# Counts by ScalarE, stacked edge-weight products and a pair mask on GpSimd in a four-block graph kernel

## The chip, the cores and the metric

One NeuronCore of a Trainium2 chip runs the whole program. The metric is the device time of one execution in microseconds (us), and the median of several runs is what counts. The engines are TensorE (PE in the profile; its weight loads are PEld), VectorE (DVE), ScalarE (ACT), GpSimd (POOL) and SyncE (SP), which here only issues DMAs. Each engine works through its own list of instructions in order, and semaphores tie the lists together. GpSimd issues the indirect DMAs.

## The reference, cut to what matters

1250 nodes with 512 values each and 20000 edges, sorted by `dst`. Four blocks follow each other, each added to its input: an equivariant graph layer, a layer of 64 experts with routing, a graph attention net of four layers, and a feed-forward layer.

```python
# block 1, the edges
h = ssp(f_ij @ W1 + b1)                      # softplus minus log 2, 32 hidden values per edge
Wij = (h @ W2 + b2) * rcut_ij[:, None]       # 4 of the 6 weights per feature are used: 128 columns
# ... products of the gathered node values with Wf and the edge's directions ...
agg = segment_sum(edge, idx_i)
# block 3, in each layer and head
scores = einsum('ehd,ehd->eh', q[src], k[dst])
attn = softmax of the scores over the edges with the same src
out = segment_sum(attn[:, :, None] * v[dst], src)
```

The kernel does block 3 densely: scores of all 1250 x 1250 pairs, with the logarithm of the number of edges of a pair as a mask, and a very large value where a pair has no edge. So block 1 also counts edges per pair, for use in block 3.

## The kernel before

Stages follow each other, each with its own semaphores and a barrier of all engines at its end: constants, input projection, **edges**, node update, **expert norm**, **route**, **experts**, the first **rows stage**, and then attention and rows stages by turns. The rest is not touched.

**edges** handles 160 tiles of 125 edges as 40 groups (`g`) of 4 tiles (`EG`); four groups (`SG`) share one computation of the hidden values. The order is written out by hand on every engine.
- TensorE: `weigh(g + 1)` makes the weights of the next group in PSUM bank 5, a bias product (L521, float32r, 33 rows) and four fp32 products with 32 rows each (L523). Then `scatter(g, j)` sums the messages onto the nodes by products with one-hot rows, in a high and a low float32r part (L538). Once in four groups `turn` (L504) and `hidden` (L512) make the next hidden values.
- VectorE: `messages(g)` multiplies weights and gathered rows (L444 to L459), compares each edge's pair key with those of its tile (`same`, L466), masks that with a triangle (`prior`, L469), makes the low part (L473), and then the index work: `early` (L476), `kd` (L477), `late_cnt` (L478), `kf` (L480) and `late_idx` (L482). `hot` (L426) builds three of four one-hot rows, `act_sum` (L431) finishes the hidden values.
- ScalarE: `high` copies the messages' high part, `hot` makes the fourth one-hot row (L387, L389), `bend` and `softplus` the hidden values, `column_sums` (L398) sums expert weights for routing.
- GpSimd: `fetch` gathers the node rows of a group by four indirect DMAs (L338). `pair_adds` (L579) adds the counts of one tile to one of two count matrices in HBM (`pairs`), each an indirect DMA with accumulation. Addition `n` waits for the landing of addition `n - 2`. 60 are spread over the first 38 groups (`PACED_ADDS`), 68 are issued in the stage (`EARLY_ADDS`), and the others stand in later stages by the tuple `LATE`: 14 in node update, 12 in expert norm, 66 in experts.
- SyncE loads `keyrow` for each group and expert weights in pieces of 512 KB.

**route** computes on VectorE which expert each row goes to; GpSimd waits for the slots and scatters ten tiles of rows to HBM (L872), and the experts stage loads them back. SyncE loads 5 MB of expert weights at the same time. **experts**: GpSimd works through its 66 additions, waits for their landing and for the stored outputs, and gathers the outputs (L1075).

**First rows stage** (`rows_stage` with `masks`): norms of ten tiles of rows, then 24 units of queries and keys (`unit(n)`, L1437), then values (L1446). TensorE makes a unit, ScalarE takes it (`take(n)`), VectorE cuts the low part of a key (`finish(n)`, L1900). Between them stands the mask work per tile of 125 x 1250 counts: VectorE adds the two matrices and takes the maximum (L1908), ScalarE takes the logarithm (L1784) and a Relu with scale -1e28 (L1786), VectorE subtracts (L1914), SyncE stores. `COUNT_AT`, `LOG_AT` and `CAP_AT` give the unit after which each step stands. Counts of tiles 6 to 9 are loaded into buffers that earlier tiles leave; in SyncE's list the conditioning weights (`late`) stand between the loads of tile 7 and the store of mask 5, and SyncE waits there until they have landed.

## Time and profile before

| | |
|---|---|
| median of 3 runs | 2878.57 us (2877.28 to 2882.2) |
| the profiled execution | 2881.81 us, its span 2880.0 us |
| busy in the span | PE 2520.4, PEld 2166.2, DVE 1861.9, ACT 1396.8, POOL 1139.5 us |
| mean granted clock of TensorE | 0.945 of full speed |
| edges | first product of the stage's weights at 78.96 us, last scatter product until 543.1 us |
| route, experts | from 623.7 and from 663.9 us |
| first rows stage | from 943.7 us, value products from 1064.13 us |

Busy times are shares of engines that wait for each other, so they don't say what a change is worth; that is read from the stretch of time in which the changed work stands. A granted clock of 1.00 in a window is 2.4 GHz, one of 0.50 is 1.2 GHz. An instruction in a timeline has its start and its length; the difference of two starts is what it takes of its engine's time, since the next begins before the last one's end is through.

### The profile page before, as it was taken

The numbers are of one execution on the slowest core, as the hardware profiler recorded it, in microseconds if no ns is written. First come the engines' busy times: TensorE is split into PE (matmuls) and PEld (weight loads), VectorE is DVE, ScalarE is ACT, GpSimd is POOL, SyncE is SP. The second block draws the span as 40 slices with busy tenths as digits, with TensorE's granted clock in tenths as the row PEclk, the third lists the DMA queues.
The fourth block names the chain that finished last, engine by engine and source line by source line (L and its number), as shares of the span: only waits on it lengthen the run. The fifth ranks groups of instructions, "written<-read, shape, count | busy, mean of one in ns | idle before, by whom it ended". The sixth has DMA issues, their size and how long they took to land. (4 is left out here: it accounts for less than half of the span.)

```text
span 2880.0 us, 38762 instructions
## 1 busy us (share of the span) xinstructions
PE 2520.4 (88%) x13585; PEld 2166.2 (75%) x13585; DVE 1861.9 (65%) x3526; ACT 1396.8 (49%) x2764; POOL 1139.5 (40%) x850
## 2 busy tenths in 40 slices
PE   3999999746766668999999999989999989998999
PEld 3788878546556557887877877978978878877997
DVE  2899999564651745767646777457776367667862
ACT  1566566422245635655436655346654356544431
POOL 2788888853673002226003243013260022363420
PEclk9999999867878789999999999999999999999999
DMA  7444344238535752102221011111022030121101
GB/s 253 89 86 86 74 91 83 20 92 268 128 91 175 196 157 62 45 1 72 68 61 46 18 55 53 52 53 36 18 71 68 20 89 19 45 82 34 56 13 35
DMA packets 172076, 220.33 MB, mean 77 GB/s; under 512 B 111791, under 2 KB 120426, under 8 KB 164465
## 3 DMA queue, kind: packets, MB, share of 16 engines
q1 hardware_dynamic: 85134, 189.35, 22.6%
q0 software_dynamic: 86752, 28.51, 5.8%
q8 instruction: 111, 1.82, 0.3%
q14 instruction: 79, 0.65, 0.1%
HBM read 177.10 MB, written 40.15 MB: 75 GB/s over the span
## 5 line engine op out<-in xcount | busy, mean ns | idle before, releaser
L2185 POOL TENSOR_SCALAR prob<-prob,rden,linked 125x1250 f32<-125x1250 f32 x160 | 223.5, 1397 | 955.6 <-DVE rden L2152 955.6
L579 POOL DMA_INDIRECT pairs<-late_cnt,late_idx x160 | 351.1, 2195 | 125.5 <-DMA pairs<-late_cnt,late_idx 75.7
L2103 ACT CAST prob_high<-ps 125x375 fp32r<-125x375 f32 (+1 forms) x480 | 231.1, 503 | 267.1 <-PE ps L2065 261.8
L2144 DVE CUSTOM_DVE_ANT_0 prob<-ps,mask 125x1250 f32<-125x1250 f32 x160 | 233.0, 1456 | 130.1 <-PE ps L2041 109.1
L2157 DVE TENSOR_TENSOR prob_low<-ps,prob_high 125x375 fp32r<-125x375 f32 (+1 forms) x480 | 269.6, 585 | 46.6 <-ACT prob_high L2103 46.6
L338 POOL DMA_INDIRECT Hg<-h_rows,dsti x160 | 230.1, 1438 | 117.3 <-issue 94.0
L2054 PE MATMUL ps<-ident,prob 125*125 125x125 f32 x1600 | 252.3, 273 | 17.3 <-POOL prob L2185 10.7
L2054 PEld LDWEIGHTS ps<-ident,prob 125*125 125x125 f32 x1600 | 232.3, 187 | 29.7 <-POOL prob L2185 22.9
L538 PE MATMUL ps<-onehot,mhi 125*128 125x512 f32 (+1 forms) x960 | 245.7, 364 | 6.1 <-DVE onehot L426 5.9
L538 PE MATMUL ps<-onehot,mlo 125*128 125x512 f32 (+1 forms) x960 | 238.8, 357 | 0.0
L2095 ACT ACTIVATE prob<-prob,top 125x1250 f32<-125x1250 f32 x160 | 214.7, 1342 | 46.3 <-DVE top L2144 37.6
L2065 PE MATMUL ps<-prob_high,v_high 125*128 125x376 f32 (+1 forms) x480 | 211.1, 440 | 4.6 <-ACT qT L2107 3.0
L2041 PE MATMUL ps<-k_high,q_high 128*125 128x512 f32 (+1 forms) x480 | 173.9, 362 | 28.5 <-DVE q_low L2133 19.0
L538 PEld LDWEIGHTS ps<-onehot,mhi 125*128 125x128 f32 x960 | 158.4, 191 | 42.6 <-issue 13.4
L538 PEld LDWEIGHTS ps<-onehot,mlo 125*128 125x128 f32 x960 | 157.5, 191 | 28.2
L2041 PE MATMUL ps<-k_low,q_high 128*125 128x512 f32 (+1 forms) x480 | 172.5, 359 | 0.0
L2041 PE MATMUL ps<-k_high,q_low 128*125 128x512 f32 (+1 forms) x480 | 171.6, 358 | 0.0
L2065 PE MATMUL ps<-prob_low,v_high 125*128 125x376 f32 (+1 forms) x480 | 169.0, 352 | 0.0
L2065 PE MATMUL ps<-prob_high,v_low 125*128 125x376 f32 (+1 forms) x480 | 169.0, 352 | 0.0
L426 DVE TENSOR_SCALAR onehot<-iota_n,srcf 125x1250 fp32r<-125x1250 int16 x120 | 121.0, 1030 | 24.3 <-PEq L71 12.1
L2041 PEld LDWEIGHTS ps<-k_high,q_high 128*125 128x125 f32 x480 | 90.9, 189 | 50.3 <-DVE q_low L2133 20.7
L2330 POOL TENSOR_SCALAR neg<-raw,qsc 128x128 bf16<-128x128 f32 x132 | 78.6, 614 | 119.3 <-DVEq L2352 119.3
(442 smaller groups left out, 5952.4 us busy)
## 6 DMA issues: line engine op xcount, KB each, us to landing
mask<-mask_d SPq DMA_DIRECT2D x40, 546.9 KB
sg_wd<-L_ffn_Wd SPq DMA_DIRECT2D x32, 512.0 KB, 7.2
w_ring<-L_ffn_Wd SPq DMA_DIRECT2D x16, 1024.0 KB, 14.8
w_ring<-L_ffn_Wu SPq DMA_DIRECT2D x16, 1024.0 KB, 5.8
pairs<-zeros POOLq DMA_DIRECT2D x18, 625.0 KB, 25.2
keyrow<-keys_d SPq DMA_DIRECT2D x40, 244.1 KB
kept<-g_d SPq DMA_DIRECT2D x40, 224.0 KB
g_d<-kept SPq DMA_DIRECT2D x30, 224.0 KB
```

The costliest lines, as they stand in the source:

```text
L338: nc.gpsimd.indirect_dma_start(Hg[:, g % 2, j, :, :].rearrange("p c f -> p (c f)"), None, h_rows[:, :], bass.IndirectOffsetOnAxis(dsti[:, ...
L426: v.tensor_scalar(onehot[:, j, :], T.iota_n[0:P, :], srcf[:, column(g, j):column(g, j) + 1], None, ALU.is_equal).then_inc(hot_ready, 1)
L538: ins = nc.tensor.matmul(agg_chunk(T, a, c), part[:, u, j, a * 128:(a + 1) * 128], onehot[:, j, n0:n0 + nn], start=first and k == 0 and c < 2,
L579: nc.gpsimd.indirect_dma_start(pairs[a][:, :], bass.IndirectOffsetOnAxis(T.E.late_idx[:, c:c + 1], 0), T.E.late_cnt[:, c:c + 1], None, com ...
L2041: ins = nc.tensor.matmul(S(u)[0:P, n0:n0 + nn], M.qr[x][:, b % 2, i * P:(i + 1) * P], M.k[y][:, h, n0:n0 + nn], start=n == 0, stop=n == 2)
L2054: ins = nc.tensor.transpose(T.ps[0:P, 3 + s % 4, i * P:(i + 1) * P], M.prob[:, (FIRST[b] + i) % RING, j * P:(j + 1) * P], T.ident[0:P, 0:P])
L2065: ins = nc.tensor.matmul(T.ps[:, 7, 0:w], M.v[x][:, j, h * DH:(h + 1) * DH], M.pt[y][:, s % 3, 0:w], start=j == 0 and n == 0, stop=j == NT ...
L2095: s.activation(M.prob[:, u % RING, :], M.prob[:, u % RING, :], ACT.Exp, bias=M.top[:, u % RING:u % RING + 1], scale=-1.0, accum_out=M.den[ ...
L2103: s.copy(M.pt[0][:, n % 3, 0:w], T.ps[0:P, 3 + n % 4, 0:w]).then_inc(high, 1)
L2144: v.tensor_tensor_reduce(M.prob[:, r, :], S(u)[0:P, 0:N], M.mask[:, it % MASKS, :], 1.0, 3.0e38, ALU.add, ALU.min, M.top[:, r:r + 1]).then ...
L2157: v.tensor_tensor(M.pt[1][:, n % 3, 0:w], T.ps[0:P, 3 + n % 4, 0:w], M.pt[0][:, n % 3, 0:w].bitcast(F32), ALU.subtract).then_inc(low, 1)
L2185: nc.gpsimd.tensor_scalar(M.prob[:, r, :], M.prob[:, r, :], M.rden[:, r:r + 1], T.linked[:, it:it + 1], ALU.mult, ALU.mult).then_inc(norme ...
```

## The change

1. **Edge weights.** The hidden values of a group are split in a high and a low part and stacked by three DMAs per group on 98 rows: high, low, high, and two rows of ones. The weights stand against them as high, high, low and the two parts of the bias. One float32r product per tile replaces bias product and fp32 product. ScalarE and VectorE prepare the stacked weights at the stage's start.
2. **Index work.** `same` and `prior` become bf16. ScalarE sums the counts of each tile (`counts`), VectorE computes `kd` once for all tiles and `kf`, `late_idx` once in four groups.
3. **Additions.** They start with group 8: 40 up to group 37, 52 in the stage. Eight now stand in route, ahead of the scatters, and 74 in experts.
4. **Pair mask.** GpSimd adds the counts, compares and subtracts. ScalarE takes the logarithm alone, and its accumulated sum tells whether a row has an edge. VectorE does one small comparison in the end.

```diff
@@ -32,8 +32,10 @@
 SG = 4
-EARLY_ADDS = 68
-PACED_ADDS = 60
+EARLY_ADDS = 52
+PACED_ADDS = 40
+PACE_FROM = 8
+STACK = 8
@@ -292,24 +294,28 @@
         pre = sb("pre", [128, EG * P]); sa = sb("sa", [128, EG * P]); se = sb("se", [128, EG * P])
-        hT = sb("hT", [128, 2, EG * P])
+        hT = sb("hT", [128, EG * P]); h_hi = sb("h_hi", [128, 2, EG * P], F32R); h_lo = sb("h_lo", [128, 2, EG * P], F32R)
+        stack = sb("h_stack", [3 * FF + 2, STACK, EG * P], F32R); w_stack = sb("w_stack", [3 * FF + 2, 128], F32R)
...
         onehot = sb("onehot", [P, EG, N], F32R); away = sb("away", [P, N]); minus = sb("minus", [P, ET])
-        keyrow = sb("keyrow", [P, 2, EG, P]); same = sb("same", [P, EG, P]); prior = sb("prior", [P, EG, P])
+        keyrow = sb("keyrow", [P, 2, EG, P]); same = sb("same", [P, 2, EG, P], BF16); prior = sb("prior", [P, EG, P], BF16)
+        lowerb = sb("lowerb", [P, P], BF16); tally = sb("tally", [P, EG, P], BF16)
...
         wd_src = A["L0_ffn_Wd"]
-        early = sb("early", [P, EG]); kd = sb("kd", [P, EG]); kf = sb("kf", [P, EG])
+        early = sb("early", [P, 2, EG, SG]); kd = sb("kd", [P, ET]); kf = sb("kf", [P, EG * SG])
...
         names = ("wd_in0 wd_in1 wd_in2 wd_in3 summed keyrow_in0 keyrow_in1 hg_in0* hg_in1* keyrow_free f_turned fT_ready h_made bent soft_step h_ready "
...
@@ -322,6 +328,18 @@
                                      keyrows_d[g // SG, g % SG:g % SG + 1, :, :].broadcast_to([P, EG, P])).then_inc(keyrow_in[g % 2], 16)
+                        if g == 0:
+                            for k in range(2):
+                                sp.dma_start(w_stack[3 * FF + k:3 * FF + k + 1, :].bitcast(F32),
+                                             E.b2[32 * k:32 * k + 1, 0, :].bitcast(F32)).then_inc(b2_in, 16)
+                        if g % SG == 0:
+                            sp.wait_ge(h_split, g // SG + 1)
+                            for r in range(SG):
+                                if g + r >= STACK:
+                                    sp.wait_ge(w_made, g + r - STACK + 1)
+                                for k, part in enumerate((h_hi, h_lo, h_hi)):
+                                    sp.dma_start(stack[k * FF:(k + 1) * FF, (g + r) % STACK, :].bitcast(F32),
+                                                 part[r * FF:(r + 1) * FF, g // SG % 2, :].bitcast(F32)).then_inc(st_in[(g + r) % STACK], 16)
@@ -345,10 +363,12 @@
                             fetch(g + 2)
-                        more = PACED_ADDS * (g + 1) // NG if g < NG - 2 else EARLY_ADDS - 4 * (NG - 1 - g)
-                        pool.wait_ge(idx_ready, more // EG + 1)
-                        pair_adds(pool, nc, T, pairs, n, more)
-                        n = more
+                        if g >= PACE_FROM:
+                            more = PACED_ADDS * (g + 1 - PACE_FROM) // (NG - PACE_FROM) if g < NG - 2 else EARLY_ADDS - 4 * (NG - 1 - g)
+                            pool.wait_ge(idx_ready, (more - 1) // (EG * SG) + 1)
+                            pool.wait_ge(tallied, EG * SG * ((more - 1) // (EG * SG) + 1))
+                            pair_adds(pool, nc, T, pairs, n, more)
+                            n = more
@@ -388,6 +408,15 @@
 
+                    def counts(g):
+                        act.wait_ge(keyrow_free, g + 1)
+                        if g >= 1:
+                            act.wait_ge(tallied, EG * g)
+                        for j in range(EG):
+                            c = column(g, j)
+                            s.activation(tally[:, j, :], same[:, g % 2, j, :], ACT.Copy,
+                                         accum_out=E.late_cnt[:, c:c + 1]).then_inc(tallied, 1)
+
@@ -396,6 +425,10 @@
                             s.activation(junk[:, k, :], wd[:, l % WRING, i, k, :], ACT.Copy, accum_out=T.E.tsum[:, e, k:k + 1]).then_inc(summed, 1)
+                    s.copy(w_stack[0:3 * FF, :], E.w2[0:3 * FF, :, :].rearrange("p k f -> p (k f)")).then_inc(w_stacked, 1)
+                    s.activation(stack[3 * FF:3 * FF + 2, :, :],
+                                 T.zeros[3 * FF:3 * FF + 2, 0:EG * P].unsqueeze(1).broadcast_to([2, STACK, EG * P]), ACT.Identity,
+                                 bias=T.ones[3 * FF:3 * FF + 2, 0:1]).then_inc(w_stacked, 1)
@@ -411,6 +444,7 @@
                         hot(g)
+                        counts(g)
@@ -428,7 +462,14 @@
                         dve.wait_ge(soft_step, 2 * q + 2)
-                        v.scalar_tensor_tensor(hT[:, q % 2, :], sa[:], -LOG2, pre[:], ALU.add, ALU.add).then_inc(h_ready, 1)
+                        if q >= 2:
+                            for r in range(SG):
+                                dve.wait_ge(st_in[(SG * q + r) % STACK], 48 * (q // 2))
+                        v.scalar_tensor_tensor(hT[:], sa[:], -LOG2, pre[:], ALU.add, ALU.add).then_inc(h_ready, 1)
+                        dve.wait_ge(h_ready, q + 1)
+                        step(v.tensor_copy(h_hi[:, q % 2, :], hT[:]))
+                        settle()
+                        v.tensor_tensor(h_lo[:, q % 2, :], hT[:], h_hi[:, q % 2, :].bitcast(F32), ALU.subtract).then_inc(h_split, 1)
@@ -463,25 +504,32 @@
                         dve.wait_ge(keyrow_in[u], (g // 2 + 1) * 16)
-                        step(v.tensor_tensor(same[:], keyrow[:, u, :, :], kcol.unsqueeze(2).broadcast_to([P, EG, P]), ALU.is_equal))
+                        if g >= 2:
+                            dve.wait_ge(tallied, EG * (g - 1))
+                        step(v.tensor_tensor(same[:, u, :, :], keyrow[:, u, :, :], kcol.unsqueeze(2).broadcast_to([P, EG, P]), ALU.is_equal))
...
                         v.sem_inc(keyrow_free, 1)
-                        step(v.tensor_tensor(prior[:], same[:], T.lower[:].unsqueeze(1).broadcast_to([P, EG, P]), ALU.mult))
+                        step(v.tensor_tensor(prior[:], same[:, u, :, :], lowerb[:].unsqueeze(1).broadcast_to([P, EG, P]), ALU.mult))
...
                         settle()
-                        step(v.tensor_reduce(early[:], prior[:], AX.X, ALU.add))
-                        step(v.tensor_scalar(kd[:], kcol, T.iota_p[:, 0:1], None, ALU.subtract))
-                        step(v.tensor_reduce(E.late_cnt[:, tiles(g)], same[:], AX.X, ALU.add))
-                        settle()
-                        step(v.scalar_tensor_tensor(kf[:], early[:], 0.0, kd[:], ALU.is_equal, ALU.mult))
-                        settle()
-                        step(v.tensor_scalar(E.late_idx[:, tiles(g)], kf[:], T.iota_p[:, 0:1], None, ALU.add))
-                        settle()
-                        v.sem_inc(idx_ready, 1)
+                        q, r = divmod(g, SG)
+                        step(v.tensor_reduce(early[:, q % 2, :, r], prior[:], AX.X, ALU.add))
+                        if r == SG - 1:
+                            c = slice(EG * SG * q, EG * SG * (q + 1))
+                            settle()
+                            step(v.scalar_tensor_tensor(kf[:], early[:, q % 2, :, :].rearrange("p j r -> p (j r)"), 0.0, kd[:, c],
+                                                        ALU.is_equal, ALU.mult))
+                            settle()
+                            v.tensor_scalar(E.late_idx[:, c], kf[:], T.iota_p[:, 0:1], None, ALU.add).then_inc(idx_ready, 1)
+                    dve.wait_ge(w_stacked, 1)
+                    v.tensor_tensor(w_stack[2 * FF:3 * FF, :], E.w2[2 * FF:3 * FF, :, :].rearrange("p k f -> p (k f)"),
+                                    w_stack[2 * FF:3 * FF, :].bitcast(F32), ALU.subtract).then_inc(w_stacked, 1)
+                    step(v.tensor_copy(lowerb[:], T.lower[:]))
+                    step(v.tensor_scalar(kd[:], key[:], T.iota_p[:, 0:1], None, ALU.subtract))
@@ -512,16 +560,15 @@
                     def weigh(g):
-                        q, r = divmod(g, SG)
-                        rows = slice(r * FF, (r + 1) * FF)
-                        if r == 0:
-                            pe.wait_ge(h_ready, q + 1)
+                        pe.wait_ge(st_in[g % STACK], 48 * (g // STACK + 1))
+                        if g == 0:
+                            pe.wait_ge(w_stacked, 3)
+                            pe.wait_ge(b2_in, 32)
...
                             pe.wait_ge(w_free, g)
-                        nc.tensor.matmul(T.ps[0:P, 5, :], E.one33[:], E.b2[:].rearrange("p j c -> p (j c)"), start=True, stop=False)
                         for j in range(EG):
-                            ins = nc.tensor.matmul(T.ps[0:P, 5, j * 128:(j + 1) * 128], hT[rows, q % 2, j * P:(j + 1) * P],
-                                                   E.w2[rows, :, :].rearrange("p k f -> p (k f)"), start=False, stop=j == EG - 1)
+                            ins = nc.tensor.matmul(T.ps[0:P, 5, j * 128:(j + 1) * 128], stack[:, g % STACK, j * P:(j + 1) * P],
+                                                   w_stack[:], start=True, stop=True)
@@ -568,7 +615,7 @@
 
-LATE = (EARLY_ADDS, EARLY_ADDS + 14, EARLY_ADDS + 26, ET)
+LATE = (EARLY_ADDS, EARLY_ADDS + 14, EARLY_ADDS + 26, EARLY_ADDS + 34, ET)
@@ -867,6 +914,7 @@
                     g.iota(ecol[:], [[0, 1]], 0, 1, **kw).then_inc(made, 1)
+                    late_adds(pool, nc, T, pairs, 2)
@@ -1081,7 +1129,7 @@
                     g.memset(T.cw[:], 0.0).then_inc(c_made, 1)
-                    late_adds(pool, nc, T, pairs, 2)
+                    late_adds(pool, nc, T, pairs, 3)
@@ -1491,15 +1539,14 @@
         self.pair_c, self.pair_m = [free[name] for name in "abcdegjfhg"], [free[name] for name in "lmkjfhabcd"]
...
 
-COUNT_AT = (3, 4, 5, 6, 8, 9, 12, 13, 15, 17)
-LOG_AT = (4, 5, 6, 7, 9, 10, 13, 14, 16, 18)
-CAP_AT = (5, 6, 8, 9, 10, 11, 14, 16, 18, 19)
-TINY, BIG = 1.0e-18, 1.0e28
+LOG_AT = (4, 4, 5, 5, 6, 7, 14, 15, 20, 21)
+TINY, BIG = 1.0e-18, 1.0e30
+UNLINKED = (N - 0.5) * math.log(TINY)
@@ -1640,8 +1687,28 @@
                 if masks:
+                    def count(t):
+                        pool.wait_ge(pair_in[t], 64)
+                        nc.gpsimd.tensor_tensor(M.pair_c[t][:], M.pair_c[t][:], M.pair_m[t][:], ALU.add).then_inc(counted, 1)
+
+                    def mask(t):
+                        pool.wait_ge(logd, t + 1)
+                        nc.gpsimd.tensor_scalar(M.pair_m[t][:], M.pair_c[t][:], -1.0, BIG, ALU.is_lt, ALU.mult).then_inc(empty, 1)
+                        pool.wait_ge(empty, t + 1)
+                        nc.gpsimd.tensor_tensor(M.pair_c[t][:], M.pair_m[t][:], M.pair_c[t][:], ALU.subtract).then_inc(mask_made, 1)
                     nc.gpsimd.memset(M.tiny[:], TINY).then_inc(consts, 1)
-                    nc.gpsimd.memset(M.far[:], -BIG).then_inc(consts, 1)
+                    for t in range(6):
+                        count(t)
+                    for t in range(6):
+                        mask(t)
+                    count(6)
+                    count(7)
+                    mask(6)
+                    mask(7)
+                    count(8)
+                    count(9)
+                    mask(8)
+                    mask(9)
@@ -1779,11 +1846,10 @@
                     if t == 0:
-                        act.wait_ge(consts, 2)
+                        act.wait_ge(consts, 1)
                     act.wait_ge(counted, t + 1)
-                    s.activation(M.pair_c[t][:], M.pair_c[t][:], ACT.Ln, bias=M.tiny[0:P, :]).then_inc(logd, 1)
-                    act.wait_ge(logd, t + 1)
-                    s.activation(M.pair_m[t][:], M.pair_c[t][:], ACT.Relu, bias=M.far[0:P, :], scale=-BIG).then_inc(capped, 1)
+                    s.activation(M.pair_c[t][:], M.pair_c[t][:], ACT.Ln, bias=M.tiny[0:P, :],
+                                 accum_out=M.pair_top[:, t:t + 1]).then_inc(logd, 1)
@@ -1900,19 +1966,6 @@
 
-                def masking(n):
-                    for t in range(NT) if masks else ():
-                        if n == COUNT_AT[t]:
-                            c = M.pair_c[t][:]
-                            dve.wait_ge(pair_in[t], 64)
-                            v.tensor_tensor_reduce(c, c, M.pair_m[t][:], 1.0, 0.0, ALU.add, ALU.max,
-                                                   M.pair_top[:, t:t + 1]).then_inc(counted, 1)
-                    for t in range(NT) if masks else ():
-                        if n == CAP_AT[t]:
-                            c = M.pair_c[t][:]
-                            dve.wait_ge(capped, t + 1)
-                            v.tensor_tensor(c, M.pair_m[t][:], c, ALU.subtract).then_inc(mask_made, 1)
-
@@ -1935,15 +1988,11 @@
                 low(NT - 2)
-                masking(3)
...
                 low(NT - 1)
-                masking(4)
-                masking(5)
...
                     finish(n)
-                    masking(n)
@@ -1952,7 +2001,8 @@
                 if masks:
-                    v.tensor_scalar(T.linked[:], M.pair_top[:], 1.0, None, ALU.min).then_inc(spare, 1)
+                    dve.wait_ge(logd, NT)
+                    v.tensor_scalar(T.linked[:], M.pair_top[:], UNLINKED, None, ALU.is_gt).then_inc(spare, 1)
```

## Rows read from the trace of the kernel before

**Rows 1.** Windows: busy us of each engine, granted clock, DMA share, GB/s

```profile
300.00:350.00 50.00, 49.54 (x259) 40.46 (x258) 46.22 (x89) 30.37 (x77) 39.73 (x26) 1.00 0.44 89
```

**Rows 2.** Timeline of TensorE over four groups: start, length, work

```profile
305.63 0.50 PE L521 MATMUL ps<-b,one 33*125 33x512 f32 x1
306.06 1.13 PE L523 MATMUL ps<-w,hT 32*125 32x128 f32 x8
307.12 0.83 PE L538 MATMUL ps<-onehot,mhi 125*128 125x512 f32 x3
...
318.53 0.80 PE L538 MATMUL ps<-onehot,mhi 125*128 125x512 f32 x3 [0.42 <-DVE onehot L426]
...
351.15 0.50 PE L521 MATMUL ps<-b,one 33*125 33x512 f32 x1
```

**Rows 3.** Timeline of VectorE, index work and hidden values

```profile
304.62 0.54 DVE L477 TENSOR_SCALAR kd<-key,iota_p 125x4 f32<-125x4 f32 x1
304.75 0.66 DVE L478 TENSOR_REDUCE late_cnt<-same 125x4 f32<-125x500 f32 x1
...
306.02 1.85 DVE L426 TENSOR_SCALAR onehot<-iota_n,srcf 125x1250 fp32r<-125x1250 int16 x2
...
341.10 0.66 DVE L431 SCALAR_TENSOR_TENSOR hT<-sa,pre 128x500 f32<-128x500 f32 x1
```

**Rows 4.** Groups by line in the edge stage: busy us, mean ns

```profile
L538 PE MATMUL ps<-onehot,mlo 125*128 125x226 f32 x317 | 85.5, 270 | 0.0
...
L398 ACT ACTIVATE sg_junk<-sg_wd 128x128 f32<-128x128 f32 x228 | 67.2, 296 | 1.6 <-ACT sg_junk L398 0.4
L389 ACT ACTIVATE onehot<-away,ones 125x1250 fp32r<-125x1250 f32 x36 | 48.3, 1343 | 1.2
```

**Rows 5.** Timeline at the edge stage's start

```profile
78.22 0.68 DVE L431 SCALAR_TENSOR_TENSOR hT<-sa,pre 128x500 f32<-128x500 f32 x1 [8.12 <-ACT sa L374]
```

**Rows 6.** Timeline at its end: 13 additions, and TensorE's last products

```profile
509.75 2.17 POOL L579 DMA_INDIRECT pairs<-late_cnt,late_idx  x1 [0.30 <-issue]
...
540.32 1.97 POOL L579 DMA_INDIRECT pairs<-late_cnt,late_idx  x1 [0.30 <-issue]
542.35 0.75 PE L538 MATMUL ps<-onehot,mlo 125*128 125x512 f32 x3
```

**Rows 7.** GpSimd in route and experts (timeline), and windows of route

```profile
640.49 1.23 POOL L872 DMA_INDIRECT xs_d<-xf,r_slot  x1 [16.09 <-DVEq L945]
666.12 2.02 POOL L579 DMA_INDIRECT pairs<-late_cnt,late_idx  x1 [0.19 <-issue]
...
693.09 1.98 POOL L579 DMA_INDIRECT pairs<-late_cnt,late_idx  x1 [13.33 <-DMA pairs<-late_cnt,late_idx]
...
723.51 1.98 POOL L579 DMA_INDIRECT pairs<-late_cnt,late_idx  x1 [5.84 <-DMA pairs<-late_cnt,late_idx]
...
636.00:640.00 4.00, 4.00 (x40) 4.00 (x40) 1.01 (x3) 0.00 (x0) 0.00 (x0) 0.50 0.98 408
640.00:644.00 4.00, 4.00 (x40) 4.00 (x40) 0.14 (x1) 0.00 (x0) 2.90 (x3) 0.50 0.35 35
```

**Rows 8.** GpSimd's wait before the gather of the outputs (timeline)

```profile
916.95 1.27 POOL L1075 DMA_INDIRECT w_ring<-y_d,r_slot  x1 [29.77 <-DMA y_d<-xs]
```

**Rows 9.** GpSimd beside VectorE in the rows stage, and GpSimd's scaling

```profile
954.63 1.26 POOL L1624 TENSOR_TENSOR set_b_low<-set_b_raw,set_b_high 128x512 fp32r<-128x512 f32 x1 [2.82 <-ACT set_b_high L1733]
954.76 1.15 DVE L1873 SCALAR_TENSOR_TENSOR shift<-mv,rstd 125x1 f32<-125x1 f32 x1
...
L2185 POOL TENSOR_SCALAR prob<-prob,rden,linked 125x1250 f32<-125x1250 f32 x160 | 223.5, 1397 | 955.6 <-DVE rden L2152 955.6
```

**Rows 10.** Rows stage: waits, the store of mask 3, the first value product

```profile
PE ps L1437 <- DVE k_low L1900: 21.5, 4, 14.0
...
1009.20 0.30 SPq L141 DMA_DIRECT2D mask_d<-pair_d  x1
...
1064.13 1.09 PE L1446 MATMUL ps<-set_b_high,y_high 128*125 128x512 f32 x4
```

12 lines of the change are left out of this document (7 added, 5 removed).

## The prediction, made before the changed kernel ran

> **What bounds the kernel now.** I read the windows first, then the groups of instructions by line, then the timeline at each place that the diff touches. From 85 to 543 us the edge stage runs, and there the windows show TensorE busy 49.5 of 50 us and VectorE 46.2, ScalarE 30.4, GpSimd 39.7 [rows 1]. The timeline shows that both are the bound: from one edge-weight product to the one four groups later TensorE takes 45.52 us, 11.38 a group, and waits once in them, 0.42 us for a one-hot of VectorE [rows 2]; and VectorE's instructions follow each other without a gap of any size [rows 3]. So the stage speeds up only by what leaves both engines. Behind it lie stages of waits: the clock is 1.2 GHz (granted 0.50) and the DMA queues are full in the routing stage [rows 7], and in the first rows stage TensorE stands idle 21.5 us for VectorE's key splits [rows 10], which are queued behind mask work that waits for its counts. GpSimd's long lists of count additions end inside the stage where they stand, at some ends with little room [rows 6, 8].
>
> **Edge stage, TensorE.** A group's weights take 1.49 us, 305.63 to 307.12: one bias product and four fp32 products, each in two instructions [rows 2]. After: four single-pass products of 128 columns. The nearest rows: eight L523 instructions fill the 1.06 us between 306.06 and 307.12, 0.13 each, so four are 0.53; above lies the one-hot product of 226 columns, single-pass too, whose 270 ns from start to end make 1.08 for four [rows 2, 4]; below, half of 0.53, were a product bound by its columns alone. With the lead of 0.2 us that now stands before the block I take 0.75: 0.74 less a group (bounds 0.2 and 1.0).
>
> **Edge stage, VectorE.** By starts in the timeline the key difference takes 0.13 us, and the count reduction with the two index steps 1.27 up to the next one-hot, of which the reduction is 0.66 and the steps 0.61 [rows 3]. The first two leave, the steps come once in four groups: 0.13 + 0.66 + 0.75 x 0.61 = 1.25 us less. The product with the triangle passes over the same 500 elements as that reduction and now has bf16 operands: unchanged, or half, 0 to 0.3 less; I take 0.1, as every row here of such a pass has the full time. Added once in four groups: a copy, a subtraction of 500 columns and two drains, each instruction at most the 0.66 us of L431 [rows 3], 1.4 us, 0.35 a group. Net 1.0 less (0.8 to 1.2): 10.4 a group. The Trainium skill, VectorE: DVE Perf Modes, section What auto-detection actually checks, says that an operation whose tensors are all 16-bit with unit step gets the mode of two results a cycle; by it the triangle product falls by some 0.3 us and the group to 10.2. No row here has that form.
>
> **Edge stage, ScalarE and GpSimd.** ScalarE gets four counts a group, each like L398 at 0.296 us [rows 4]: 1.2 us more on 6.9, by its 30.4 of 50 us [rows 1]. In the group that also has the softplus (with two table loads 5.2 us) its copy for the message split comes about 1.5 us late; once in four groups, 0.1 to 0.4 us a group if nothing hides it. I take a period of 10.5 us, 0.85 less (0.5 to 1.0). Over the 37 groups up to the last fetch: 31.5 us. GpSimd has 4 fetches of 1.75 and 1.25 additions of 2.6 a group, 10.3 us: just inside.
>
> **Start of the edge stage.** ScalarE first copies the stacked weights and fills 4000 ones per partition. A 1250-column activation takes 1343 ns [rows 4], so 4.3 us, before the features. The hidden rows, now at 78.22 us [rows 5], then need a copy, a subtraction and three transfers (about 3 us) before the first product. Of both 6 us reach the path (4 to 8).
>
> **End of the edge stage.** After the last fetch GpSimd has 13 additions now, 509.75 to 542.29, 2.50 each, and TensorE ends at 543.1 [rows 6]. With PACED_ADDS 40 and EARLY_ADDS 52 the 37th group stands at 37, the next at 48, the last at 52: 16 additions, 40.0 us, where TensorE now needs 33.3 and then 31. So GpSimd becomes the bound of the stage's end and 6.7 us come back. Edge stage: -31.5 + 6 + 6.7 = -18.8 us (-28 to -8).
>
> **Routing.** Eight additions come in ahead of the row scatters. GpSimd idles 16.09 us there [rows 7]; at 2.27 us each, the free pace, eight take 18.2, so the scatters start at least 2.1 us later, and nothing covers them. But SyncE's 5 MB of expert weights start with them, and the queues carry 408 GB/s until 640 us, then 35 [rows 7]. An addition waits for the landing of the last but one; under such a load in the next stage these waits were up to 13.33 us [rows 7]. So I take it that two pairs land by about 640 and the others follow: the first scatter at 650 instead of 640.49, +10 us (2 to 17). Queued behind are the ten scatters, and TensorE waits for these rows.
>
> **Experts.** 74 additions in place of 66. GpSimd then waits 29.77 us for the stored outputs [rows 8]; eight more at 2.5 us, 20, fit. Cost 0; if each takes over 3.6 us, the rest shows.
>
> **First rows stage.** VectorE loses 20 passes of 1.45 us, ScalarE ten of 1.34. GpSimd gets per tile an addition (nearest row 1.26 us for 512 columns [rows 9], so 3.0 for 1250), a comparison (as L2185, 1.4 [rows 9]) and a subtraction: 7.4 us, 74 in all. The masks are needed late, so that the path becomes: mask 3 frees a buffer, counts 6 and 7 are loaded, then the conditioning rows, then counts 8 and 9, then the last count and logarithm, and only then does ScalarE split the value weights. Mask 3, whose store is issued at 1009.20 now, would be ready at about 1005 (six counts, from the last weight split at 963 on, and then 4.5 us a mask from the first logarithm at 987 on), so the chain runs some 4 us earlier; after its last load it has 3.0 + 1.5 + 2.2 + 0.6 us, and no key products behind it. It ends near 1056, where the value products now start at 1064.13 [rows 10]: 8 us less. Against this: where GpSimd works on SBUF, VectorE's tiny instruction with two SBUF operands at 954.76 lasts 1.15 us, to the end of GpSimd's that began at 954.63; alone it takes 0.16 [rows 9]. GpSimd is now busy throughout, and four such scale steps and the eight weight splits meet it; the last four splits are on the path, and each can wait up to 2.8 us. I take 5 us of it: -3 us for the stage (-10 to +5). The Trainium skill, SBUF — State Buffer, section Who interferes with whom, says that a VectorE instruction with two SBUF inputs and a GpSimd one that reads SBUF block each other whole; the trace agrees with its 1.15 us. Its GPSIMD Engine Reference, section Engine selection, advises VectorE for elementwise work, at about half GpSimd's time for two inputs; by the rows it is 1.45 against about 3.0 us.
>
> **Sum** against the profiled execution (span 2880.0, 2881.8 with what lies around it): -18.8 + 10 - 3 = -11.8 us, 2870.0. The median of the runs is 3.2 us lower, so 2866.8 us.
>
> **Rivals.** (1) Routing swamps it: if all eight additions go at the pace of the first eight of the expert stage, 666.12 to 723.51 us, 7.2 each [rows 7], they take 57 us against 16 idle, +41, and the end is 2878.6 - 18.8 - 3 + 41 = 2898. It decides from 4.7 us an addition on (+22). For it: the queues are full when they start. Against it: they are full for only 15 us. Chance 0.12. (2) The gain is handed back: the period falls only to 10.7 us, because VectorE waits for ScalarE's late copies, and the blocked splits cost the rows stage all its gain: 37 x 0.68 = 25.2, less 12.7 at start and end, 10 for routing and 0 in the rows stage leave 2.5, or 2876, with 2873 to 2884 around it. For it: ScalarE's queue is in order, and the long softplus stands ahead of the counts; against it: VectorE shows no wait for ScalarE now. Chance 0.16. The port rule of the skill leads here too. (3) More than I think: narrow products at 0.1 us, the period at 10.3, routing at its low bound, the rows stage at -8: -26 + 2 - 8 = -32, 2847. Chance 0.12. (4) The forecast, 2854 to 2873: 0.60.
>
> **How the numbers follow.** Changes within 0.2% (5.8 us) can't be told from none here. Faster: forecast and (3) and a little of (2), 0.72; same, most of (2) and the upper end of the forecast, 0.15; slower, (1) and a rest of (2), 0.13. The range, 2848 to 2883, leaves out (1) and the far end of (3); the forecast's own is 2854 to 2873.
>
> **What would show it.** In the changed profile: group period 10.5 us by the product's starts; four products in under 0.6 us; GpSimd's additions outlasting TensorE in the edge stage by 5 to 10 us; the first row scatter some 30 us or less after the routing stage's iotas, not 16; GpSimd without a long wait before its additions' end in the expert stage; value products near 1061 on the old scale, with VectorE's splits stretched to over 1 us. Wrong if the products take four times their columns, if ScalarE's late copies stall VectorE each group, or if additions in routing pass 4.7 us.

## The result, and the profile after

The changed kernel takes 2898.47 us (median of 8 runs, 2891.91 to 2903.65), the kernel before 2880.39 us beside it (8 runs): ratio 1.006, 95% interval 1.0047 to 1.0074. It is 18 us slower; the forecast was 2866.8 us, and the result lies outside its range of 2848 to 2883. The profiled executions are 21.9 us apart (spans 2901.9 and 2880.0; the changed kernel's is the slowest of its eight). All differences below are between profiled executions, by the start of the same instruction in both.

The windows over the stretch of [rows 1], in the changed kernel (busy us of each engine, clock, DMA share, GB/s):

```profile
300.00:350.00 50.00, 47.56 (x252) 40.10 (x252) 44.17 (x81) 36.14 (x120) 38.66 (x26) 1.00 0.49 106
```

TensorE's timeline there, the products of four groups, and its two stalls (these lines answer to [rows 2]):

```profile
307.35 0.55 PE L570 MATMUL ps<-w_stack,h_stack 98*125 98x128 f32 x4
307.74 0.78 PE L585 MATMUL ps<-onehot,mhi 125*128 125x512 f32 x3
317.91 0.55 PE L570 MATMUL ps<-w_stack,h_stack 98*125 98x128 f32 x4
327.58 0.56 PE L570 MATMUL ps<-w_stack,h_stack 98*125 98x128 f32 x4
329.52 0.80 PE L585 MATMUL ps<-onehot,mhi 125*128 125x512 f32 x3 [1.38 <-DVE onehot L460]
339.26 0.55 PE L570 MATMUL ps<-w_stack,h_stack 98*125 98x128 f32 x4
340.87 0.81 PE L585 MATMUL ps<-onehot,mhi 125*128 125x512 f32 x3 [1.06 <-DVE onehot L460]
350.20 0.56 PE L570 MATMUL ps<-w_stack,h_stack 98*125 98x128 f32 x4
```

Four groups take 42.85 us, 10.71 a group against 11.38. Four products cost 0.39 us (307.35 to 307.74) in place of 1.49 for the bias product and the fp32 products. But TensorE, which stood still once for 0.42 us in four groups, now stands still twice, 1.38 and 1.06 us by the brackets. Why shows in the timelines of ScalarE and VectorE ahead of the first stall:

```profile
318.40 0.72 ACT L394 ACTIVATE sa<-se,ones 128x500 f32<-128x500 f32 x1
319.02 1.33 ACT L407 ACTIVATE away<-iota_n,minus 125x1250 f32<-125x1250 int16 x1
320.38 1.34 ACT L409 ACTIVATE onehot<-away,ones 125x1250 fp32r<-125x1250 f32 x1
325.28 1.03 ACT L400 CAST mhi<-msg 125x1024 fp32r<-125x1024 f32 x1
326.34 1.23 DVE L516 TENSOR_TENSOR mlo<-msg,mhi 125x1024 fp32r<-125x1024 f32 x1 [2.24 <-ACT mhi L400]
```

Read it from below: VectorE waits 2.24 us for ScalarE's high copy; ScalarE has no gap before that copy, since the softplus, two one-hot steps, four counts and eight column sums stand in its queue. What VectorE loses there makes its next one-hots late, and TensorE waits for those.

The end of the edge stage and the routing stage, GpSimd's timeline (these answer to [rows 6] and [rows 7]):

```profile
488.69 1.51 POOL L356 DMA_INDIRECT Hg<-h_rows,dsti  x1 [0.30 <-issue]
490.50 2.19 POOL L626 DMA_INDIRECT pairs<-late_cnt,late_idx  x1 [0.30 <-issue]
...
526.97 1.96 POOL L626 DMA_INDIRECT pairs<-late_cnt,late_idx  x1 [0.30 <-issue]
532.97 1.97 POOL L626 DMA_INDIRECT pairs<-late_cnt,late_idx  x1 [4.04 <-issue]
...
610.89 0.18 POOL L911 IOTA w<- 125x64 f32 x1 [2.79 <-POOLq L73]
...
626.25 1.98 POOL L626 DMA_INDIRECT pairs<-late_cnt,late_idx  x1 [10.18 <-DMA pairs<-late_cnt,late_idx]
...
641.86 1.21 POOL L920 DMA_INDIRECT xs_d<-xf,r_slot  x1 [0.30 <-issue]
...
905.58 1.96 POOL L626 DMA_INDIRECT pairs<-late_cnt,late_idx  x1 [0.30 <-issue]
918.49 1.27 POOL L1123 DMA_INDIRECT w_ring<-y_d,r_slot  x1 [10.95 <-DMA y_d<-xs]
```

TensorE's last product of the edge stage runs from 518.82 to 519.57, GpSimd's additions to 528.93. So they outlast TensorE by 9.4 us, where before they ended 0.8 us ahead of it. The next stage's first addition is at 532.97, where it was at 546.81: the edge stage yields 13.8 us. The eight additions in routing put the first scatter 31.0 us after the iotas, which was 16.7 us before; the third waited 10.18 us for the landing of the first, while the windows from 614 to 626 us show a DMA share of 0.97 to 1.06. The experts begin at 663.94, before the change at 663.95: up to here nothing is won and nothing lost. GpSimd's idle time ahead of the gather fell from 29.77 to 10.95 us, so the longer list is hidden: the gather starts 1.5 us later.

The first rows stage, GpSimd's mask work in its timeline, with lines of VectorE, ScalarE, SyncE and TensorE in the order of time (these answer to [rows 9, 10]):

```profile
967.77 2.84 DVE L1939 SCALAR_TENSOR_TENSOR shift<-mv,rstd 125x1 f32<-125x1 f32 x1
...
993.82 4.48 POOL L1696 TENSOR_SCALAR pair_l<-pair_a 125x1250 f32<-125x1250 f32 x1 [8.07 <-ACT pair_a L1851]
998.38 2.88 POOL L1698 TENSOR_TENSOR pair_a<-pair_l,pair_a 125x1250 f32<-125x1250 f32 x1
1001.34 4.44 POOL L1696 TENSOR_SCALAR pair_m<-pair_b 125x1250 f32<-125x1250 f32 x1
...
1002.72 11.12 DVE L1922 TENSOR_TENSOR set_a_low<-set_a_raw,set_a_high 128x512 fp32r<-128x512 f32 x4 [6.04 <-ACT set_a_high L1800]
...
1024.37 0.30 SPq L143 DMA_DIRECT2D mask_d<-pair_d  x1
...
1042.00 1.34 ACT L1851 ACTIVATE pair_j<-pair_j,tiny 125x1250 f32<-125x1250 f32 x1 [17.46 <-POOL pair_j L1692]
...
1071.20 10.51 DVE L1922 TENSOR_TENSOR set_b_low<-set_b_raw,set_b_high 128x512 fp32r<-128x512 f32 x4 [3.44 <-ACT set_b_high L1800]
...
1081.77 2.07 PE L1494 MATMUL ps<-set_b_high,y_high 128*125 128x512 f32 x4 [9.79 <-DVE set_b_low L1922]
```

The last four splits in the kernel before:

```profile
1061.35 2.49 DVE L1856 TENSOR_TENSOR set_b_low<-set_b_raw,set_b_high 128x512 fp32r<-128x512 f32 x4
```

The comparison with its product takes 4.44 us where I had taken 1.4, and from 993.82 to 1060 us GpSimd works with hardly a gap. Mask 3 is stored at 1024.37 in place of 1009.20. The two four-part weight splits of VectorE take 11.12 and 10.51 us. The value products start at 1081.77 (before: 1064.13), and at half their speed, 2.07 us for four in place of 1.09, after 9.79 us of waiting: the first value row is 19.4 us later. Of that 2.2 us were there when the stage's norms began, so the stage lost 17.2 us.

The path to the first value row has three parts. From GpSimd's first weight split to VectorE's last four splits it takes 118.4 us in place of 110.8: 7.6 us, the mask chain. From there to the value products it takes 10.6 us in place of 2.8: 7.8 us, the stretched splits. From there to the first value row it takes 4.8 us in place of 3.0: 1.8 us, the slow products. Their clock shows it: granted 0.73 from 1080 to 1090 us, after the long wait, and 1.00 from 1060 to 1070 in the kernel before.

Through the four attention stages the distance wanders between 16.7 and 21.9 us, and 21.9 is what is left at the end.

### The profile page after: what moved, and what is told of

It reads as the page before. It is cut to its first block and busy times, and to the rows that moved or that the text cites. A ratio compares the mean times of both kernels' runs of the same rounds, so it can differ in the third digit from the quotient of the medians.

```text
span 2901.9 us, 38782 instructions
## 1 busy us (share of the span) xinstructions
PE 2471.7 (85%) x13385; PEld 2136.3 (74%) x13385; DVE 1820.5 (63%) x3379; ACT 1434.2 (49%) x3086; POOL 1219.2 (42%) x879
## 5 line engine op out<-in xcount | busy, mean ns | idle before, releaser
L626 POOL DMA_INDIRECT pairs<-late_cnt,late_idx x160 | 341.8, 2136 | 136.9 <-DMA pairs<-late_cnt,late_idx 87.2
L356 POOL DMA_INDIRECT Hg<-h_rows,dsti x160 | 219.2, 1370 | 163.8 <-issue 91.0
L2104 PE MATMUL ps<-ident,prob 125*125 125x125 f32 x1600 | 252.3, 273 | 17.2 <-POOL prob L2235 10.6
L585 PE MATMUL ps<-onehot,mhi 125*128 125x512 f32 (+1 forms) x960 | 244.9, 363 | 22.8 <-DVE onehot L460 21.2
L460 DVE TENSOR_SCALAR onehot<-iota_n,srcf 125x1250 fp32r<-125x1250 int16 x120 | 113.5, 967 | 6.2 <-DVE v L488 0.7
## 6 DMA issues: line engine op xcount, KB each, us to landing
w_ring<-L_ffn_Wd SPq DMA_DIRECT2D x16, 1024.0 KB, 13.3
```

The lines of the kernel that those rows point to most:

```text
L356: nc.gpsimd.indirect_dma_start(Hg[:, g % 2, j, :, :].rearrange("p c f -> p (c f)"), None, h_rows[:, :], bass.IndirectOffsetOnAxis(dsti[:, ...
L585: ins = nc.tensor.matmul(agg_chunk(T, a, c), part[:, u, j, a * 128:(a + 1) * 128], onehot[:, j, n0:n0 + nn], start=first and k == 0 and c < 2,
L626: nc.gpsimd.indirect_dma_start(pairs[a][:, :], bass.IndirectOffsetOnAxis(T.E.late_idx[:, c:c + 1], 0), T.E.late_cnt[:, c:c + 1], None, com ...
L2104: ins = nc.tensor.transpose(T.ps[0:P, 3 + s % 4, i * P:(i + 1) * P], M.prob[:, (FIRST[b] + i) % RING, j * P:(j + 1) * P], T.ident[0:P, 0:P])
```

## The experiments

Each kernel ran beside the kernel before on one chip. The column "rows stage" is the time from GpSimd's first weight split to VectorE's first value row in the profile, which leaves out what came earlier.

| kernel | median us | ratio to before, 95% interval | rows stage us | four value-weight splits us |
|---|---|---|---|---|
| before | 2880.39 | | 116.6 | 2.49 |
| changed | 2898.47 | 1.006 (1.0047 to 1.0074) | 133.8 | 10.51 |
| e1 old mask | 2885.36 | 1.0012 (1.0 to 1.0024) | 117.1 | 2.49 |
| e2 mask alone | 2894.65 | 1.0045 (1.0028 to 1.0061) | 129.9 | 10.51 |
| e3 product and maximum | 2897.09 | 1.0051 (1.0035 to 1.0068) | 131.5 | 10.38 |
| e5 the same, scalars from columns | 2893.7 | 1.0042 (1.0027 to 1.0056) | 126.6 | 6.93 |
| e9 two products from columns | 2885.44 | 1.0013 (1.0001 to 1.0025) | 114.9 | 5.68 |
| e4 routing without additions | 2906.45 | 1.0085 (1.0067 to 1.0103) | | |
| e10 stacked products alone | 2903.44 | 1.0064 (1.0042 to 1.0087) | | |
| e11 index work and additions | 2896.44 | 1.0047 (1.0033 to 1.0061) | | |
| e6 e1, ScalarE relieved | 2873.41 | 0.9968 (0.9952 to 0.9983) | | |
| e7 e1, additions moved | 2870.26 | 0.9955 (0.9937 to 0.9973) | | |
| e8 e6 and e7 | 2857.9 | 0.9914 (0.9897 to 0.993) | 116.6 | 2.49 |
| e12 e8, add and subtract on GpSimd | 2850.43 | 0.9906 (0.9889 to 0.9922) | 110.9 | 4.73 |

**e1, part 4 undone.** The hunks of the mask in the diff, taken backward:

```diff
-LOG_AT = (4, 4, 5, 5, 6, 7, 14, 15, 20, 21)
+COUNT_AT = (3, 4, 5, 6, 8, 9, 12, 13, 15, 17)
+LOG_AT = (4, 5, 6, 7, 9, 10, 13, 14, 16, 18)
+CAP_AT = (5, 6, 8, 9, 10, 11, 14, 16, 18, 19)
```

> The changed kernel with part 4 undone: mask work on VectorE and ScalarE as before, the rest as changed. Theory A (the loss is the mask on GpSimd: value products 19.4 us later in the changed profile, of which 2.2 us were there before the stage's norms): about 17 us faster than the changed kernel, 2881 us, level with the kernel before; the mask back gives first value products near 1068 us. Rival (the loss sits in the additions, in the DMA load or in a lower clock of later stages): it stays above 2890 us.

2885.36 us: 13 us of the loss are the mask. The rival, which asked for more than 2890 us, falls. That it is not quite level with the kernel before was not expected; in this profile the edge stage's first product also came 3.0 us later than in that of the changed kernel, which no edit explains (see the end of the next section).

**e2, part 4 alone**, on the kernel before, the same hunks forward.

> The kernel before with part 4 alone. Theory A: 17 us slower than before, about 2897 us, value products 17 us later than in the kernel before. Rival (the mask costs only because it meets what parts 1 to 3 changed): within 4 us of the kernel before.

2894.65 us, 15 above the kernel before; its rows stage takes 13.3 us more. The mask costs by itself, whatever stands ahead of it.

**e3, another operation.**

```diff
-tensor_scalar(M.pair_m[t][:], M.pair_c[t][:], -1.0, BIG, ALU.is_lt, ALU.mult)
+tensor_scalar(M.pair_m[t][:], M.pair_c[t][:], -1.0e28, 0.0, ALU.mult, ALU.max)
```

> The changed kernel, where GpSimd's comparison with -1 and product with 1e30 (4.44 us each) becomes a product with -1e28 and a maximum with 0 (a node pair without an edge still gets a very large value). Theory A1 (the operation's price is what the prediction had wrong, and the stores and loads of the mask chain hang on it): the instruction takes 1.4 us like the scaling of the attention, a mask 4.3 instead of 7.5 us, mask 3 is stored 12 us earlier, and with the later masks 15 to 19 us come back: 2880 to 2884 us. Theory A2 (GpSimd blocks VectorE's splits whatever it computes): the splits stay at 2 to 3 us each, mostly waiting, and only about 8 us come back: 2890 us. Theory A3 (any such pass of GpSimd takes 4.4 us): no change.

The instruction takes 4.43 us again, and the time is that of the changed kernel within 2 us: A3 came. A1 is wrong as I had put it: a comparison is not dearer than a product with a maximum.

**e5, the scalars from columns**, on e3's operation; `far` and `nil` are columns of -1e28 and 0.

```diff
-tensor_scalar(M.pair_m[t][:], M.pair_c[t][:], -1.0, BIG, ALU.is_lt, ALU.mult)
+tensor_scalar(M.pair_m[t][:], M.pair_c[t][:], M.far[0:P, 0:1], M.nil[0:P, 0:1], ALU.mult, ALU.max)
```

> The changed kernel, whose mask operation on GpSimd is the product with -1e28 and the maximum with 0 again, but both scalars are now read from a column per partition, as the scaling of the attention reads its own. Theory B1 (scalars that stand in the instruction are what makes the pass 4.44 us long; the attention's scaling of the same shape takes 1.40): the pass takes 1.4 us, a mask 4.3, and with it 5 to 12 us of the 13 to 15 that the mask costs come back: 2888 us. Theory B2 (comparisons and maxima are slow, products are not): 4.4 us again, no change from 2898 us. VectorE's four-part splits, 11.1 and 10.5 us now, fall to about 6 by B1, since GpSimd reads SBUF less of the time.

Of this kernel, GpSimd's and VectorE's timelines:

```profile
997.22 4.58 POOL L1697 TENSOR_SCALAR pair_m<-pair_b,far,nil 125x1250 f32<-125x1250 f32 x1
998.54 7.72 DVE L1926 TENSOR_TENSOR set_a_low<-set_a_raw,set_a_high 128x512 fp32r<-128x512 f32 x4 [6.04 <-ACT set_a_high L1804]
```

B1 is wrong: 4.58 us, even a little more. Yet VectorE's splits fell from 11.0 (e3) to 7.7 us and the stage by 4.9 us, with a GpSimd pass that is no shorter. So how long VectorE is kept waiting depends also on the form of GpSimd's instruction, and not on its length alone. What in the form does it, no run shows.

**e9, the very operation of the attention's scaling**: as e5, with `ALU.mult, ALU.mult` and a column of 1. This kernel leaves out the maximum, so its masks are not the reference's.

> The changed kernel, whose mask operation on GpSimd is two products with columns, the very operation of the attention's scaling (1.40 us for the same shape); the maximum with zero is left out, so pairs of nodes with several edges get another mask than the reference's. Theory D1 (it is the comparison or maximum that GpSimd does slowly, products are fast): the pass takes 1.4 us, a mask 4.3, mask 3 is stored near 1010 us, and the time is what the prediction's price would have given: 2884 to 2888 us, still above the kernel before, since VectorE's splits are stretched. Rival D2 (the pass is slow in this stage whatever it computes, because the engines beside it use SBUF, or because it writes another buffer than it reads): 4.4 us again and 2894 us.

```profile
989.07 1.39 POOL L1697 TENSOR_SCALAR pair_l<-pair_a,far,nil 125x1250 f32<-125x1250 f32 x1 [8.08 <-ACT pair_a L1855]
...
1018.37 2.82 POOL L1693 TENSOR_TENSOR pair_j<-pair_j,pair_a 125x1250 f32<-125x1250 f32 x1 [1.38 <-DMA pair_a<-pairs]
...
1054.68 5.68 DVE L1926 TENSOR_TENSOR set_b_low<-set_b_raw,set_b_high 128x512 fp32r<-128x512 f32 x4 [3.38 <-ACT set_b_high L1804]
```

1.39 us. D1 holds: with the same scalars, buffers and neighbours, product and maximum take 4.6 us and two products 1.4. GpSimd now waits for loads again, where in the changed kernel the loads waited for GpSimd. The rows stage takes 1.7 us less than before the change; my forecast for it was 3 less. By the three parts above, against before: 6.5 us less up to the last splits, 3.0 more for the splits, 1.8 more for the slow products. Against e5, where only the second operation differs, 10.0 of 11.7 us are won ahead of the last splits. Two of its ten product passes took 2.87 us, both while VectorE's four splits ran: GpSimd was kept waiting too.

**e4, routing without additions.**

```diff
-LATE = (EARLY_ADDS, EARLY_ADDS + 14, EARLY_ADDS + 26, EARLY_ADDS + 34, ET)
+LATE = (EARLY_ADDS, EARLY_ADDS + 14, EARLY_ADDS + 26, EARLY_ADDS + 26, ET)
```

> The changed kernel with the eight additions of the routing stage moved to the end of the experts' list (82 there). Theory: the row scatters start 14 us earlier, near 627.6 us, the experts 13 us earlier; the longer list then ends about 19 us later relative to the stage, of which the 11 us of idle before the gather hide a part, so that 8 us are exposed and the gain is 3 to 6 us: 2894 us. Rival 1 (all hidden): 13 us faster, 2885 us. Rival 2 (additions under the expert weights' load are slower than 3.5 us each): no gain or a loss.

```profile
629.86 1.23 POOL L919 DMA_INDIRECT xs_d<-xf,r_slot  x1 [16.09 <-DVEq L992]
...
917.43 1.97 POOL L626 DMA_INDIRECT pairs<-late_cnt,late_idx  x1 [0.30 <-issue]
922.01 1.27 POOL L1122 DMA_INDIRECT w_ring<-y_d,r_slot  x1 [2.62 <-issue]
```

The routing stage behaves as expected: GpSimd waits 16.09 us for the slots, and the experts begin 11.5 us earlier, at 652.46. But the list of 82 ends at 919.40, where the outputs are ready 254.5 us after the stage's start, near 907. Eight additions took 23 us there, 2.9 each, with 11 us to hide in; with the last one's landing 15 us are exposed, where I had expected 8, and the gather comes 3.5 us later than in the changed kernel. The norms start 4.3 us later, and the profiled execution is as much longer; the medians are 8 us apart, and the rest isn't explained. The outcome is rival 2's, a loss, though the additions are not as slow as it said. They must stand neither in routing nor behind the 74.

**e10, the stacked products alone**, the hunks of `stack`, `w_stack`, `h_hi`, `h_lo` and `weigh` on the kernel before, and **e11, parts 2 and 3 alone**, the changed kernel with the old mask and the old `weigh`.

> The kernel before with the stacked single-pass products alone; index work, additions and mask as before. Theory (both engines were the bound, VectorE with 46.2 us of 50 and no gap of any size): with 1.1 us a group off TensorE and 0.35 us a group more on VectorE the period goes from 11.38 to 11.3 to 11.6 us, and the start costs 7 us: 2880 to 2893 us, no gain. Rival (TensorE alone was the bound): period 10.6 us, 2858 us.

> The changed kernel with the old mask and the old edge-weight products: index work and counts as changed, additions as changed (eight in the routing stage). Theory: TensorE keeps its 11.38 us, so the period does not fall; with the additions' own cost of 13 us in routing and a stage end that is TensorE's again, 2885 to 2895 us. Rival (VectorE alone was the bound): period 10.6, 2878 us.

Windows of e10 and, behind it, of e11:

```profile
300.00:350.00 50.00, 45.76 (x233) 38.35 (x232) 46.29 (x91) 30.93 (x85) 40.14 (x25) 0.97 0.45 89
```

```profile
300.00:350.00 50.00, 50.00 (x262) 40.93 (x261) 40.64 (x75) 35.91 (x117) 38.52 (x25) 1.00 0.43 93
```

In e10 VectorE stays at 46.3 us of 50 and TensorE falls to 45.8: the period over 32 groups rises from 11.37 to 11.66 us, TensorE waits 31.7 us for one-hots between 100 and 480 us, and its granted clock falls from 1.00 to between 0.93 and 0.97 in windows of 50 us. In e11 TensorE is busy all the time and VectorE has room; the period is 11.24 us. Neither half shortens the period by more than 0.15 us, both together do so by 0.64 (to 10.74): two engines were the bound, as the first part of the prediction had read it. The times were worse than expected: e10 is 10 us above its 2880 to 2893, of which the period, above the 11.6 us allowed for, gives 2 and the first product, 10.6 us late and not 7, gives 4; e11 is 1 us above its bound, and its edge stage still ends with GpSimd's additions, 6.6 us behind TensorE.

**e6, ScalarE relieved in the edge stage** (on e1): no column sums in the softplus group, and its counts behind the next high copy. The two edits were not run apart.

```diff
                         high(g)
+                        if g >= 1 and soft[g - 1]:
+                            counts(g - 1)
...
-                        counts(g)
-                        for e in range(NX * max(g - 1, 0) // (NG - 1), NX * g // (NG - 1)):
-                            column_sums(e)
+                        if not soft[g]:
+                            counts(g)
+                        if g in rest:
+                            k = rest.index(g)
+                            for e in range(NX * k // len(rest), NX * (k + 1) // len(rest)):
+                                column_sums(e)
```

> The changed kernel with the old mask (2885 us) and two edits on ScalarE in the edge stage: no column sums in the group that has the softplus (the other groups take them), and that group's counts stand behind the next group's high copy. Theory C1 (TensorE's stalls of 2.8 us in four groups come from ScalarE's late high copy, 2.24 us, which makes VectorE late for the low part and the next one-hots): the period falls from 10.74 to about 10.1 us and TensorE's part of the stage ends 20 us earlier; but GpSimd's additions end the stage, so the whole gains only a few us. Rival C2 (VectorE's own work is the bound): period unchanged, no gain.

The chain of waits from 100 to 480 us by line (us in total, times, longest), first of the changed kernel, then of e6:

```profile
DVE mlo L516 <- ACT mhi L400: 21.5, 14, 2.8
PE ps L585 <- DVE onehot L460: 20.5, 17, 1.9
```

```profile
DVE mlo L523 <- ACT mhi L400: 4.4, 6, 1.9
PE ps L592 <- DVE onehot L467: 3.0, 5, 1.1
```

In e1, which e6 edits, the first wait is 21.3 us and the second 15.1. Both shrink together, and the period over 32 groups falls from 10.74 to 10.34 us, not to 10.1: TensorE still stands idle for 8.7 us there, 0.24 a group, of which 5.5 have no releaser in the profile. C1 holds in kind. TensorE's part of the stage ends 13 us earlier, not 20, yet the whole gained 12 us against e1, more than "a few", because GpSimd's last fetch, and with it its list, came 13 us earlier too.

**e7, additions moved** (on e1), and **e8, e6 and e7 together**.

```diff
-EARLY_ADDS = 52
-PACED_ADDS = 40
-PACE_FROM = 8
+EARLY_ADDS = 60
+PACED_ADDS = 50
+PACE_FROM = 4
...
-LATE = (EARLY_ADDS, EARLY_ADDS + 14, EARLY_ADDS + 26, EARLY_ADDS + 34, ET)
+LATE = (EARLY_ADDS, EARLY_ADDS + 14, EARLY_ADDS + 26, EARLY_ADDS + 26, ET)
```

> The changed kernel with the old mask and another placement of the additions: they start with group 4, 50 up to group 37 and 60 in the edge stage, none in the routing stage, 74 in the experts' as changed. Theory: the end of the edge stage is TensorE's again, 6 to 8 us earlier, and the row scatters start 14 us earlier within the routing stage; the experts' list, equally long, ends as late after its start as now, with some 10 us of idle left: 20 us faster than with the old mask alone, 2865 us. Rival (GpSimd has no room in the edge stage: fetches are late): the period rises over 10.8 us and half of it is lost, 2875 us.

> The last two together. Theory: TensorE's period near 10.1 us now shows, as GpSimd's list no longer ends the stage: 2850 us. Rival (GpSimd, with 6.65 us of fetches and 1.4 additions of 2.45 us a group, is full at 10.1 us): the period stays at 10.4 or more, 2858 us.

e7 gains 15 us against e1, e8 27; expected were 20 and 35. In both the first scatter is 16.7 us after the iotas as before the change, and in e8 GpSimd still idles 11.24 us ahead of the gather. What failed in both expectations is the end of the edge stage. In e8:

```profile
508.56 0.75 PE L592 MATMUL ps<-onehot,mlo 125*128 125x512 f32 x3
516.57 1.98 POOL L633 DMA_INDIRECT pairs<-late_cnt,late_idx  x1 [0.30 <-issue]
523.10 1.96 POOL L633 DMA_INDIRECT pairs<-late_cnt,late_idx  x1 [4.55 <-issue]
```

GpSimd's list still ends the stage: 15 additions stand behind the last fetch, where e1 and e6 have 16, and they outlast TensorE by 9.2 us (8.0 in e7). The next stage begins at 523.10, in e6 at 523.36. So the moved additions gain only the routing stage's 14 us, and the 9.2 us at the stage's end are about the 8 us by which e8 misses its 2850; that they are the whole cause is an estimate. The rival's number, 2858 us, came true, but not its mechanism: the period is 10.36 us, as in e6 with fewer additions, and GpSimd waits 15.1 us for VectorE between 100 and 480 us, so it is not full. e8 is 22 us faster than the kernel before.

**e12, a third mask** (on e8's edge stage).

```diff
-                        pool.wait_ge(logd, t + 1)
-                        nc.gpsimd.tensor_scalar(M.pair_m[t][:], M.pair_c[t][:], -1.0, BIG, ALU.is_lt, ALU.mult).then_inc(empty, 1)
...
                                  accum_out=M.pair_top[:, t:t + 1]).then_inc(logd, 1)
+                    act.wait_ge(logd, t + 1)
+                    s.activation(M.pair_m[t][:], M.pair_c[t][:], ACT.Relu, bias=M.far[0:P, :], scale=-BIG).then_inc(empty, 1)
```

> The kernel of e8 (lighter softplus group, additions moved, 2858 us) with a third form of the mask: GpSimd only adds the counts and subtracts (2.85 us each), ScalarE takes the logarithm and the Relu as before the change, nothing is compared on GpSimd. Theory (the slow comparison was the whole of the mask's loss, the blocked splits a smaller rest): a mask every 2.9 us instead of 7.4, the value products within 3 us of those of the old mask, 2854 to 2860 us. Rival (what GpSimd does at all beside VectorE's norms and splits costs as much as it frees): 2865 us or more.

2850.43 us, 0.9906 of the kernel before (0.9889 to 0.9922). That is 4 us below the 2854 to 2860 expected. Its rows stage is 5.7 us shorter than the old one. The splits take 4.7 us, so the block by GpSimd is still there, but it costs less than the freed VectorE passes give. Against e8 the two intervals overlap. In the profiles e12 is 30.5 us ahead of the kernel before at the first attention's scaling and 22.3 at the last, e8 23.4 and 22.8, though the code between is the same, and the profiled execution of e12 is 7 us above its median: whether e12 beats e8 is not settled.

## Why the prediction was wrong, point by point

- **What bounds the edge stage**: right. e10 and e11 show each engine's half by itself.
- **TensorE's product slot** 1.49 to 0.75 us: it fell to 0.39. That is 1.10 us less, just beyond the bound of 1.0. Each product took 0.10 us, less than the 0.13 of the old ones' instructions; the far row of 226 columns had pulled my value up.
- **VectorE**, 1.0 us less a group: 44.17 busy us of 50 at 10.71 are 9.46 a group, 10.52 before, so 1.06. The triangle product fell from 698 to 422 ns with bf16 operands; the Trainium skill's rule (VectorE: DVE Perf Modes, What auto-detection actually checks) gave 0.3 us where I took 0.1, and the trace agrees with the rule.
- **ScalarE**: four counts cost 1.17 us (1.2 foretold), the high copy is late in the softplus group (2.24 us for my 1.5). But I let this cost 0.1 to 0.4 us a group; TensorE's two stalls make 0.6 a group, where its one stall made 0.1 before, because VectorE passes the delay on to the next group's one-hots. Period 10.71 instead of 10.5: this is rival (2)'s place and size. From the third group's products to the last group's, the 37 groups gave 26.8 us for 31.5 foretold.
- **Start of the edge stage**, +6: the first product came 7.3 us later, the third 4.9. The fill of ones took 3.62 us, and the hidden values came 2.9 us later; the way from them to the product took 5.15 us (0.74 before).
- **End of the edge stage**, +6.7: 8.1 us, what is left of the stage's sum; the 16 additions took 38.4 us for the 40.0 foretold, by the mechanism foretold. The stage: -13.8 us for -18.8, within its bounds.
- **Routing**, +10 (2 to 17): the first scatter 14.2 us later relative to the iotas, the experts 12.9. Right in kind, with the wait for a landing under full queues (10.18 us). Rival (1) asked for 41 us and did not come.
- **Experts**, 0: 1.5 us.
- **First rows stage**, -3 (-10 to +5): +17.2. **This is the step that failed**, and within it one term, "a comparison (as L2185, 1.4)". L2185 was a row of the right engine, shape and instruction, but of two products; the operation with a comparison takes 4.44 us. "4.5 us a mask" became 7.5, mask 3 was not ready at 1005 but 1024, and GpSimd itself became the chain: up to the last splits +7.6 us where -8 was foretold. The first logarithm's result also came 4.6 us later than the 987 taken, on the scale of before (2.3 us in e9). e9 puts the foretold price in its place and gets -1.7 us for the stage, near the -3 foretold. There the block on the path cost 3.0 us, within the 5 taken; in the changed kernel it cost 7.8, so the slow operation took part in that too. The 1.8 us of slow products stood in no term. The Trainium skill (SBUF — State Buffer, Who interferes with whom) foretells the block, and 2.5 us turned into 10.5 agree with it; that the loss varies with the form of GpSimd's instruction at the same operation (10.4 us in e3, 6.9 in e5) it doesn't tell.
- **The whole miss.** The profiles differ from the sum by 33.7 us: 20.2 in the first rows stage, 5.0 in the edge stage, 2.9 in routing, 3.2 in the stages between, and 2.5 in the later stages, whose code is unchanged. With the rows stage as foretold the median would lie near 2878 us. But e9, with the foretold price of the operation, measured 2885.44 us and e1, without the new mask, 2885.36: both are above the range as well. So the comparison is the largest wrong term, and not the only one.
- **Range and rivals.** No rival had a slower GpSimd operation. The price of a comparison was a value that no row of before showed, and I gave it one row and no upper bound. The addition of two tensors, at 3.0 us, was already twice that row; even with that as its bound a mask would have been priced at 6 us, and it took 7.5.

What stays open: why product with maximum is slow and two products are fast on GpSimd; whether a comparison with its scalars in columns would be faster, which was not run; and the wandering of the later rows stages by up to 5 us, and of the edge stage's start by up to 4, between profiled executions of the same code, which blurs every comparison of single profiles by that much.

## What to carry to other kernels

Price an operation that moves to another engine by its own kind: engine, shape and instruction name agreed here, and the arithmetic inside made a factor of three. When work goes to an idle engine, add up its whole chain against the times at which its results are needed, before counting what it frees; and give each price without a row an upper bound. An engine's spare time also has an order: eight additions cost about 1 us in the edge stage (e7 against e1), 14 us in routing and 15 at the end of the experts' list. In ScalarE's queue, counts and column sums ahead of the copy that others wait for cost TensorE two stalls, until they stood elsewhere.
